# Norm steps and a bias addition of an attention stage put on GpSimd, the relu as one VectorE instruction

## The chip, the core and the metric

One core of one Trainium2 chip runs the whole program. Time is the device time of one execution in microseconds (us); the median of the runs counts. The core has five instruction queues: PE (TensorE, matmuls; PEld is its weight load), DVE (VectorE), ACT (ScalarE), POOL (GpSimd) and SP (SyncE, which here only issues transfers). Each runs its own queue in order and waits for the others by semaphores.

## The reference

Two layers. The first is a differential attention (8 heads of 16 rows of q and k, 4 batches of 512 tokens) beside a small attention over the batch and a mixture of 8 experts. The second is a four-layer state-space scan and a second mixture. The change touches only the first layer's attention and its experts. Of the experts it is this that matters:

```python
def _moe(x, Wg, W1, b1, W2, b2):
    ...
    idx = jnp.argmax(logits, axis=-1)
    for e in range(E):
        m = (idx == e)[:, None].astype(xf.dtype)
        h = jax.nn.relu(xf @ W1[e] + b1[e])
        out = out + m * (h @ W2[e] + b2[e])
```

The attention forms two softmaxes for each head, divides each by its sum of exponentials, weighs the second by minus lambda, adds the two and then normalizes by the root of the mean square over the head's 16 channels.

## The kernel before

The stage under study (`st2`, lines 631 to 1087) does two things at once. It walks through the 8 heads, and between the heads' steps it puts the 24 expert blocks of 128 tokens.

**Passes, units, steps.** `pair_of_heads` handles two heads in 32 steps. A unit is four steps, one batch of one head (512 queries against 4 x 128 keys), so there are eight units in a pass. The first pass has no expert blocks (it works out which tokens go to which block, `route`); the next two run in a hardware loop (`Fori`) and the last one is unrolled. Each unit of these three passes has one expert block: 24 in all.

**A step.** PE computes `bank_d` (`difference`, L817) and the two halves of `bank_l` (`scores`, L822, L823); ACT makes the gate `gt` by a tanh (L932); DVE makes the two sums `tt` (L988, L989); ACT takes the exponentials of two steps at once into `ex` (L939). `bank_d` and `bank_l` have two buffers each.

**The rest of a unit.** PE weighs the values with the exponentials of the unit before (`weigh`, L863, into `bank_pv`), in two halves; ACT copies `bank_pv` into `pvs` (`keep`, L944); PE transposes it back (`turn`, L871); DVE sums it into `ybig` (`settle`, L996), and only then may PE begin the next values.

**An expert block.** SP loads the block's tokens; PE transposes them (L838); ACT copies them to `xbT` (L948); PE computes the hidden layer in four matmuls of 128 columns (`hidden`, L844, into `bank_e`); DVE does bias and relu into `hid` (`relu`, L1004); PE multiplies by the second matrix (`block_out`, L850, the stationary operand is `hid`); ACT copies the result out (L953) and SP stores it. The weights come by an indirect transfer that GpSimd issues two blocks ahead (`gather_weights`), once `block_out` is done with the buffer.

**The order** is written by hand, one queue per engine. In a unit PE's order is: transpose the block, first half of the values, two differences, `hidden`, scores, second half of the values, scores, two differences, `block_out`, scores, `turn`, scores. DVE has the four steps' sums with `settle` after the second and the relu after the fourth. GpSimd has the copies for the next head (`next_head`) and the gathers.

**The norm.** `norm_head` handles one finished head on DVE in six small steps, one after each of the steps 5 to 10 and 21 to 26 of a pass: reciprocal of the sums (L1053), times minus lambda (L1057), values times reciprocals (128x512, L1059), sum of the two halves (L1061), square (L1063), sum over the channels (L1065). Each waits on the semaphore `s_hn` for the one before. The stage after this one handles the last head.

**Loads of heads.** q and k of a head are stacked in the memory of two idle tiles, `XT` and `GATE`, by 12 transfers a head on SP (`load_part`, L107, L109).

Of the kernel before, what the change touches and what calls it, by code (L numbers as in the profile page):

```python
# [7 lines left out]
ALU = mybir.AluOpType  # L8
# [3 lines left out]
P = 128  # L12
# [35 lines left out]
def build_stages(nc, A, out):  # L48
    keep = ExitStack()
    with keep:  # L50
# [24 lines left out]
        with keep0:  # L75
# [556 lines left out]
            with st2:  # L632
# [44 lines left out]
                s_hn = sem("head_norm_steps")  # L677
# [9 lines left out]
                loaded = lambda q, k: q * (8 * PER) + 16 * (k // 2 + 1)  # L687

                with nc.Block() as block:
                    @block.sync  # L690
                    def _(sp):
# [52 lines left out]
                    def _(pool):  # L744
# [12 lines left out]

                        def next_head(q, i):
# [15 lines left out]
                        pool.sem_inc(s_cur, LEAD)  # L774
# [9 lines left out]
                        next_head(-1, 0)  # L784
                        next_head(-1, 1)

                        def turn(q, more):
# [190 lines left out]
                    def _(dve):  # L978
                        for s in (s_T, s_yb, s_relu):
                            dve.sem_inc(s, LEAD)  # L980
# [67 lines left out]
                        def norm_head(h, n, settled, done):  # L1048
                            seg = ybig[:, :, bass.ds(h * 34, 34)].rearrange("p t (s c) -> p t s c", s=2)
                            plus, minus = seg[:, :, 0, 0:16], seg[:, :, 1, 0:16]  # L1050
                            if n == 0:
                                dve.wait_ge(s_yb, settled)
                                nc.vector.reciprocal(rz[:, :, :].unsqueeze(3), seg[:, :, :, 16:17]).then_inc(s_hn, 1)  # L1053
                                return
                            dve.wait_ge(s_hn, done + n)
                            if n == 1:
                                nc.vector.tensor_scalar(rz[:, :, 1], rz[:, :, 1], neg_lam[:, :], None, ALU.mult).then_inc(s_hn, 1)  # L1057
                            if n == 2:
                                TT(seg[:, :, :, 0:16], seg[:, :, :, 0:16], rz[:, :, :].unsqueeze(3).broadcast_to([P, NT, 2, 16]), ALU.mult).then_inc(s_hn, 1)  # L1059
                            if n == 3:  # L1060
                                TT(plus, plus, minus, ALU.add).then_inc(s_hn, 1)  # L1061
                            if n == 4:
                                TT(ysq[:, :, :], plus, plus, ALU.mult).then_inc(s_hn, 1)  # L1063
                            if n == 5:
                                nc.vector.tensor_reduce(ms[:, :, bass.ds(h, 1)], ysq[:, :, :].unsqueeze(2), AX.X, ALU.add).then_inc(s_hn, 1)  # L1065

                        def pair_of_heads(q, first=False):
                            for st in range(STEPS):
# [4 lines left out]
                                if 5 <= st < 11 and not first:  # L1073
# [1512 lines left out]
```

## Time and profile before

| | |
|---|---|
| median of 3 runs | 1316.74 us (1316.6 to 1319.15) |
| the profiled execution | 1318.12 us |
| its span | 1316.3 us |
| PE, DVE, ACT, POOL busy | 87%, 84%, 79%, 69% of the span |
| mean granted clock of PE | 0.953 |
| POOL in the slices of 33 us from 165 to 329 us | 1 tenth |

The span runs from the first to the last instruction of the program; the profiled execution's own time has what lies around it too. Busy shares are means over stages with different limits; the attention stage fills some 104 to 342 us. In the rows below a time stands from the span's start; "idle before" is the idle time of that engine just ahead of the row, and the name behind the arrow is what ended it.

### The profile page before, as it was taken

Reading aid. Unit: us, or ns where it says so; the run is one execution under the profiler, and the core shown is the slowest. Engines: PE = TensorE matmul, PEld = TensorE weight load, DVE = VectorE, ACT = ScalarE, POOL = GpSimd, SP = SyncE. Lnnn points to the kernel's source line nnn. Section 1 sums busy time; section 2 is a strip of 40 time slices with the busy share of each in tenths; the row PEclk is TensorE's granted clock in tenths of the full one; section 3 lists DMA queues with packets and bytes.
Section 4 is the critical chain, followed back from the end, with each engine's and each line's share of the span. In section 5 each row is a group of like instructions: output and inputs, shape, how many; then the busy total and the mean of one; then the engine's idle time right before and its main releaser. Section 6 shows DMA issues by size and latency. Waiting matters only on the chain. (4 is left out here: it accounts for less than half of the span.)

```text
span 1316.3 us, 21647 instructions
## 1 busy us (share of the span) xinstructions
PE 1145.7 (87%) x6667; PEld 611.3 (46%) x6667; DVE 1101.3 (84%) x1535; ACT 1043.2 (79%) x1804; POOL 912.4 (69%) x749
## 2 busy tenths in 40 slices
PE   6566799999719999977999999999999999999885
PEld 4461244444515656753444444444444444444442
DVE  8967899999675323339999999999999999999997
ACT  4346999999452224378999999999999999999992
POOL 6733311111473451367999999999999999999995
PEclk9786999999858999998999999999999999999998
DMA  2022233433108216434144414442442354234420
GB/s 71 33 88 95 77 107 113 126 114 104 31 23 287 88 36 163 129 85 101 54 107 106 99 45 104 104 98 56 104 112 68 74 107 113 59 77 105 107 65 16
DMA packets 89060, 120.19 MB, mean 91 GB/s; under 512 B 17869, under 2 KB 49464, under 8 KB 88576
## 3 DMA queue, kind: packets, MB, share of 16 engines
q1 hardware_dynamic: 82688, 101.59, 30.4%
q0 software_dynamic: 6272, 17.38, 4.5%
q8 instruction: 48, 0.79, 0.3%
q14 instruction: 52, 0.43, 0.1%
HBM read 92.28 MB, written 27.45 MB: 91 GB/s over the span
## 5 line engine op out<-in xcount | busy, mean ns | idle before, releaser
L2104 POOL TENSOR_TENSOR hcm<-hs,Cc 128x1024 f32<-128x1024 f32 x255 | 600.3, 2376 | 27.8 <-DVE hs L2487 19.8
L2487 DVE TENSOR_TENSOR_SCAN hs<-decay,dbx 128x512 f32<-128x512 f32 x512 | 586.9, 1201 | 25.6 <-ACT decay L2380 9.9
L2221 PEld LDWEIGHTS dbx<-ident_sb,scaled 128*128 128x128 f32 x2048 | 227.4, 142 | 288.7 <-DVE hs L2487 164.8
L2221 PE MATMUL dbx<-ident_sb,scaled 128*128 128x128 f32 x2048 | 312.1, 283 | 41.6 <-DVE hs L2487 38.2
L2362 ACT ACTIVATE scaled<-duT,BT 128x256 f32<-128x256 f32 x579 | 266.9, 506 | 0.2 <-PE dbx L2221 0.2
L2380 ACT ACTIVATE decay<-dtr_even,a_all 128x512 f32<-128x512 f32 x256 | 179.0, 723 | 3.0 <-DVE hs L2487 1.7
L2380 ACT ACTIVATE decay<-dtr_odd,a_all 128x512 f32<-128x512 f32 x256 | 177.7, 719 | 2.4 <-DMA dtr_odd<-dt_turn 1.5
L2239 PE MATMUL y_bank<-hcm,fold_sb 128*32 128x512 f32 x1024 | 138.9, 615 | 1.8 <-POOL hcm L2104 1.8
L939 ACT ACTIVATE ex<-tt 128x2048 f32<-128x2048 f32 x64 | 123.8, 1934 | 2.5 <-DVE tt L989 1.8
L2152 PE MATMUL slots<-XT,w_tap 128*128 128x512 f32 (+1 forms) x224 | 115.5, 597 | 3.1 <-DVE scaled L2478 2.9
L988 DVE TENSOR_TENSOR tt<-bank_l,gt 128x512 f32<-128x512 f32 x128 | 87.1, 681 | 12.7 <-ACT gt L932 10.9
L2089 POOL TENSOR_SCALAR scaled<-duT,BT 128x256 f32<-128x256 f32 x204 | 95.3, 479 | 0.0
L932 ACT ACTIVATE gt<-bank_d,dgh 128x512 f32<-128x512 f32 x128 | 82.7, 714 | 10.2 <-PE bank_d L817 9.2
L989 DVE SCALAR_TENSOR_TENSOR tt<-bank_l,gt 128x512 f32<-128x512 f32 x128 | 87.1, 680 | 0.0
L1849 DVE TENSOR_TENSOR hid<-sil,u_bank 128x512 f32<-128x512 f32 x32 | 22.0, 687 | 59.1 <-ACT sil L1706 37.5
L863 PE MATMUL bank_pv<-ex,v_head 128*32 128x512 f32 x512 | 69.1, 612 | 2.0 <-DVE ybig L996 1.7
L752 POOL CAST weight_rows<-w_row 128x1 uint32 (+1 forms) x24 | 4.7, 195 | 95.1 <-PE bank_e L850 95.1
L2478 DVE TENSOR_TENSOR scaled<-slots,BT 128x1024 f32<-128x1024 f32 (+1 forms) x60 | 67.9, 1131 | 0.0
L1706 ACT ACTIVATE sil<-g_bank 128x512 f32<-128x512 f32 x32 | 19.1, 597 | 47.3 <-PE u_bank L1563 47.2
L1939 DVE TENSOR_TENSOR hid<-sil,u_bank 128x320 f32<-128x320 f32 x32 | 15.6, 488 | 48.8 <-ACT sil L1792 48.8
L1527 POOL DMA_INDIRECT shares_of_tokens<-eo,to_u x18 | 17.2, 954 | 51.9 <-ACT eo L1829 48.3
L1519 POOL DMA_INDIRECT expert_rows<-XR,rows_u x32 | 31.3, 978 | 30.9 <-PE o_bank L1570 21.6
(379 smaller groups left out, 1882.3 us busy)
## 6 DMA issues: line engine op xcount, KB each, us to landing
Cc<-bc_turn SPq DMA_DIRECT2D x256, 64.0 KB, 2.2
dtr_even<-dt_turn SPq DMA_DIRECT2D x32, 512.0 KB, 8.7
dtr_odd<-dt_turn SPq DMA_DIRECT2D x32, 512.0 KB, 8.3
dt_turn<-dt SPq DMA_DIRECT2D x16, 512.0 KB, 2.8
hid<-in_conv_row SPq DMA_DIRECT2D x4, 512.0 KB, 5.4
shares_of_tokens<-zeros SPq DMA_DIRECT2D x2, 1024.0 KB, 7.9
w_rg<-in_w_rg SPq DMA_DIRECT2D x8, 256.0 KB, 3.0
w_ru<-in_w_ru SPq DMA_DIRECT2D x8, 256.0 KB, 3.8
```

Of the source, the lines that this page charges most:

```text
L932: nc.scalar.activation(gt[:, st % RING, :], bank_d[st % 2][:, :], ACT.Tanh, scale=dgh[:, i:i + 1]).then_inc(s_G, 1)
L939: nc.scalar.activation(ex[:, (st // 4) % 2, j:j + 2, :, :], tt[:, i:i + 2, :, :], ACT.Exp).then_inc(s_E, 2)
L988: nc.vector.tensor_tensor(tt[:, st % RING, 0, :], bank_l[st % 2][:, 0, :], gt[:, st % RING, :], ALU.add)
L989: nc.vector.scalar_tensor_tensor(tt[:, st % RING, 1, :], bank_l[st % 2][:, 1, :], -1.0, gt[:, st % RING, :], ALU.mult, ALU.subtract).then_ ...
L2089: nc.gpsimd.tensor_scalar(scaled[buffer_of(l, n, k)][:, kk, :, j, :], duT[:, n % 2, kk, :].rearrange("p (g c) -> p g c", c=32), BT[:, n % ...
L2104: nc.gpsimd.tensor_tensor(hcm[:, r - 1:r + 1, :], hs[:, p % HR - 1:p % HR + 1, :], Cc[:, k:k + 1, :].broadcast_to([P, 2, 512]), ALU.mult). ...
L2152: last = mm(dst[h][:, d:512], w_tap[:, 3 - d, P * h:P * h + P], XT[:, n % 4, 0:512 - d], start=(d == 0), stop=(d == 3))
L2221: last = nc.tensor.transpose(dbx[bank_of[p]][:, P * kk:P * kk + P], scaled[buffer_of(l, b, k)][:, kk, g, :, :].rearrange("p j c -> p (j c) ...
L2239: last = mm(y_bank[h][32 * q:32 * q + 32, :], fold[:, :], hcm[:, ring_of(l, b, p + q), :], start=False, stop=(k == 3), tile_position=(0, 3 ...
L2362: nc.scalar.activation(scaled[buffer_of(l, n, k)][:, kk, :, j, :], duT[:, n % 2, kk, :].rearrange("p (g c) -> p g c", c=32), ACT.Copy, sca ...
L2380: nc.scalar.activation(dec[:, p % DR, :], dtr[b % 2][:, g, :], ACT.Exp, scale=a_all[:, l, 4 * g + k:4 * g + k + 1]).then_inc(s_dec, 1)
L2487: nc.vector.tensor_tensor_scan(hs[:, p % HR, :], dec[:, p % DR, :], dbx[bank_of[p]][:, :], 0.0, ALU.mult, ALU.add).then_inc(s_sc, 1)
```

## The change

- **Relu.** `relu` was four DVE instructions of 128x128, each adding the bias (one number per partition) and taking the maximum with 0. Now `floor_at_bias` is one DVE instruction over 128x512: max(hidden, -b1), where the bias is spread along the innermost axis. A new GpSimd step `add_bias` adds b1 to it, in place. Since max(h, -b) + b = max(h + b, 0), the value is the same. `s_relu`, for which `block_out` waits, is now raised by GpSimd, and a new semaphore `s_floor` goes from DVE to GpSimd.
- **Norm.** Of the six steps DVE keeps the first and the last: `inverse_sums` at steps 5 and 21, `mean_square` at steps 14 and 30. The four between are `weigh_head` on GpSimd, after the add of the blocks k = 2 and k = 6, ahead of the gather.
- **SP.** The loads of the first head of the second pass stand ahead of the wait for the 16 scatters, and no longer behind it.

```diff
@@ sync
                         for part in range(2):
                             load_part(sp, 1, 1, part, s_ld[1])
+                        for part in range(2):
+                            first_head_of_next(-1, part)
                         sp.wait_ge(s_scat, 16 * NT)
                         for i in range(AHEAD):
                             load_block(i, i)
-                        for part in range(2):
-                            first_head_of_next(-1, part)
@@ gpsimd
+                        def weigh_head(h, done):
+                            seg = head_values(h)
+                            plus, minus = seg[:, :, 0, 0:16], seg[:, :, 1, 0:16]
+                            pool.wait_ge(s_hn, done)
+                            pool.sem_inc(s_asked, 1)
+                            nc.gpsimd.tensor_scalar(rz[:, :, 1], rz[:, :, 1], neg_lam[:, :], None, ALU.mult).then_inc(s_hn, 1)
...
+                            nc.gpsimd.tensor_tensor(seg[:, :, :, 0:16], seg[:, :, :, 0:16], rz[:, :, :].unsqueeze(3).broadcast_to([P, NT, 2, 16]), ALU.mult).then_inc(s_hn, 1)
...
+                            nc.gpsimd.tensor_tensor(plus, plus, minus, ALU.add).then_inc(s_hn, 1)
...
+                            nc.gpsimd.tensor_tensor(ysq[:, :, :], plus, plus, ALU.mult).then_inc(s_hn, 1)
...
                         next_head(-1, 0)
+                        weigh_head(0, 1)
                         next_head(-1, 1)
+
+                        def add_bias(q, k):
+                            pool.wait_ge(s_floor, blk(q, k + 1))
+                            pool.sem_inc(s_asked, 1)
+                            nc.gpsimd.tensor_tensor(hid[:, :, :], hid[:, :, :], b1[k % 2].unsqueeze(2).broadcast_to([P, 4, P]), ALU.add).then_inc(s_relu, 1)
 
                         def turn(q, more):
                             for k in range(PER):
+                                add_bias(q, k)
+                                if k == 2:
+                                    weigh_head(q * 2 + 1, q * 12 + 7)
                                 if k == PER // 2 and more:
                                     next_head(q, 0)
+                                if k == 6:
+                                    weigh_head(q * 2 + 2, q * 12 + 13)
                                 if more or k + AHEAD < PER:
@@ vector
-                        def relu(q, k):
+                        def floor_at_bias(q, k):
                             dve.wait_ge(s_h, blk(q, k + 1))
                             dve.wait_ge(s_wl[k % 2], loaded(q, k))
-                            for f in range(4):
-                                last = nc.vector.tensor_scalar(hid[:, f, :], bank_e[:, f, :], b1[k % 2][:, f:f + 1], 0.0, ALU.add, ALU.max)
-                            last.then_inc(s_relu, 1)
+                            nc.vector.scalar_tensor_tensor(hid[:, :, :], b1[k % 2].unsqueeze(2).broadcast_to([P, 4, P]), -1.0, bank_e[:, :, :],
+                                                           ALU.mult, ALU.max).then_inc(s_floor, 1)
...
+                                if st == 5 and not first:
+                                    inverse_sums(q * 2 + 1, unit(q, 0))
+                                if st == 14 and not first:
+                                    mean_square(q * 2 + 1, q * 12 + 11)
+                                if st == 21:
+                                    inverse_sums(q * 2 + 2, unit(q, 4))
+                                if st == 30:
+                                    mean_square(q * 2 + 2, q * 12 + 17)
                                 if mb == 3 and not first:
-                                    relu(q, u)
+                                    floor_at_bias(q, u)
```

DVE's queue in unit 1 of a pass in the loop, before. L988 and L989 are a step's sums, L1053 to L1059 the norm's first three steps, L1004 the relu; ISA and REGISTER_ALU rows make up addresses and wait values:

```order
L996 TENSOR_REDUCE ybig<-bank_pv 128x4x34
L1053 ISA
L1053 RECIPROCAL rz<-ybig 128x32
L985 REGISTER_ALU
L988 TENSOR_TENSOR tt<-bank_l,gt 128x512
L989 SCALAR_TENSOR_TENSOR tt<-bank_l,gt 128x512
L1055 ISA
L1057 TENSOR_SCALAR rz<-rz,neg_lam 128x16
...
L1059 TENSOR_TENSOR ybig<-ybig,rz 128x16x2x16
L1001 REGISTER_ALU
L1004 TENSOR_SCALAR hid<-bank_e,expert_weights 128x128 x4
```

The same place in the changed kernel, where L1018 and L1019 are the sums and L1033 is the new maximum:

```order
L1026 TENSOR_REDUCE ybig<-bank_pv 128x4x34
L1079 ISA
L1079 RECIPROCAL rz<-ybig 128x32
L1015 REGISTER_ALU
L1018 TENSOR_TENSOR tt<-bank_l,gt 128x512
L1019 SCALAR_TENSOR_TENSOR tt<-bank_l,gt 128x512
...
L1031 REGISTER_ALU
L1033 SCALAR_TENSOR_TENSOR hid<-expert_weights,bank_e 128x512
```

Two norm steps are gone from between the sums, and one instruction stands for the relu's four.

GpSimd's queue in the loop, before, from the gather of one block to the next (L752 casts the row numbers, L755 issues the transfer):

```order
L752 COPY weight_rows<-w_row 128x1
L753 REGISTER_ALU
L755 DMA expert_weights<-in_w_expert,weight_rows 128x1028
L752 ISA
L752 COPY weight_rows<-w_row 128x1
L753 REGISTER_ALU
L755 DMA expert_weights<-in_w_expert,weight_rows 128x1028
```

And in the changed kernel, from the add of block k = 2 to the gather behind it:

```order
L810 TENSOR_TENSOR hid<-hid,expert_weights 128x512
L763 ISA
L765 TENSOR_SCALAR rz<-rz,neg_lam 128x16
...
L768 TENSOR_TENSOR ybig<-ybig,rz 128x16x2x16
...
L771 TENSOR_TENSOR ybig<-ybig 128x16x16
L772 REGISTER_ALU
L774 TENSOR_TENSOR ysq<-ybig 128x256
L754 ISA
L754 COPY weight_rows<-w_row 128x1
L755 REGISTER_ALU
L757 DMA expert_weights<-in_w_expert,weight_rows 128x1028
```

An add now stands ahead of each gather, and behind two adds of a pass stand the norm's four middle steps.

## Rows read from the trace of the kernel before

**Rows 1.** Windows, 10 us: busy us (instructions) per engine, clock, DMA share, GB/s.

```profile
270.00:280.00 10.00, 9.94 (x72) 4.91 (x71) 9.46 (x21) 9.18 (x13) 1.20 (x2) 1.00 0.34 99
```

**Rows 2.** Timeline of PE, last pass: start, us, engine, line, operation, count, idle before.

```profile
283.35 1.05 PE L844 MATMUL bank_e<-block_inT,expert_weights 128*128 128x128 f32 x8
...
286.42 1.05 PE L850 MATMUL bank_e<-expert_weights,hid 128*128 128x128 f32 x8
...
290.36 1.06 PE L844 MATMUL bank_e<-block_inT,expert_weights 128*128 128x128 f32 x8
...
293.43 1.14 PE L850 MATMUL bank_e<-expert_weights,hid 128*128 128x128 f32 x8
```

**Rows 3.** Timeline of PE's weight loads, same stretch.

```profile
286.21 1.08 PEld L850 LDWEIGHTS bank_e<-expert_weights,hid 128*128 128x128 f32 x8
...
293.41 0.97 PEld L850 LDWEIGHTS bank_e<-expert_weights,hid 128*128 128x128 f32 x8 [0.31 <-DVE hid L1004]
```

**Rows 4.** Timeline of DVE, same stretch.

```profile
284.45 1.13 DVE L1004 TENSOR_SCALAR hid<-bank_e,expert_weights 128x128 f32<-128x128 f32 x4
...
288.90 0.35 DVE L1053 RECIPROCAL rz<-ybig 128x32 f32<-128x32 f32 x1
...
291.05 0.68 DVE L989 SCALAR_TENSOR_TENSOR tt<-bank_l,gt 128x512 f32<-128x512 f32 x1
291.64 0.68 DVE L1059 TENSOR_TENSOR ybig<-ybig,rz 128x512 f32<-128x512 f32 x1
292.24 1.12 DVE L1004 TENSOR_SCALAR hid<-bank_e,expert_weights 128x128 f32<-128x128 f32 x4
...
297.88 0.41 DVE L1065 TENSOR_REDUCE ms<-ysq 128x16 f32<-128x256 f32 x1
```

**Rows 5.** Timeline of ACT: its copy of bank_pv, one a unit.

```profile
153.93 0.78 ACT L944 ACTIVATE pvs<-bank_pv 128x512 f32<-128x512 f32 x1
161.95 0.60 ACT L944 ACTIVATE pvs<-bank_pv 128x512 f32<-128x512 f32 x1 [0.25 <-PE bank_pv L863]
...
263.94 0.60 ACT L944 ACTIVATE pvs<-bank_pv 128x512 f32<-128x512 f32 x1 [0.47 <-PE bank_pv L863]
271.66 0.60 ACT L944 ACTIVATE pvs<-bank_pv 128x512 f32<-128x512 f32 x1 [0.54 <-PE bank_pv L863]
278.78 0.60 ACT L944 ACTIVATE pvs<-bank_pv 128x512 f32<-128x512 f32 x1 [0.28 <-PE bank_pv L863]
...
292.80 0.60 ACT L944 ACTIVATE pvs<-bank_pv 128x512 f32<-128x512 f32 x1 [0.17 <-PE bank_pv L863]
300.60 0.60 ACT L944 ACTIVATE pvs<-bank_pv 128x512 f32<-128x512 f32 x1 [0.54 <-PE bank_pv L863]
```

**Rows 6.** POOL by line: duration ns min/median/max; the third from groups, busy and mean.

```profile
L386 POOL TENSOR_TENSOR prod<-mh x16: 1257/1268/1447, 20.4 to 42.0; 128x512 f32<-128x512 f32 x16
L393 POOL TENSOR_TENSOR prod<-mh,att x16: 1042/1046/1788, 47.5 to 80.2; 128x512 f32<-128x512 f32 x16
L1508 POOL TENSOR_TENSOR hid<-tap_in,hid 128x256 f32<-128x256 f32 x12 | 8.5, 737 | 20.0 <-DMA hid<-in_conv_row 20.0
```

**Rows 7.** Timeline of PE and POOL where the third pass begins.

```profile
226.23 1.06 PE L863 MATMUL bank_pv<-ex,v_head 128*32 128x512 f32 x8
227.99 1.05 PE L850 MATMUL bank_e<-expert_weights,hid 128*128 128x128 f32 x8
...
227.50 0.18 POOL L746 COPY dgh<-delta_gain_sb 128x1 f32 x1 [3.69 <-PE bank_pv L863]
227.63 0.39 POOL L749 COPY v_head<-v_tok 128x256 f32 x1
```

**Rows 8.** Timeline of SP and PE: the third head's loads and the wait for them.

```profile
143.01 1.91 SPq L107 DMA_DIRECT2D XT<-qk_parts  x3
...
159.96 0.61 PE L817 MATMUL bank_d<-XT 112*128 112x512 bf16 x2 [2.27 <-DMA XT<-qk_parts]
```

**Rows 9.** Timeline of PE in the last unit of the last pass.

```profile
336.24 1.16 PE L850 MATMUL bank_e<-expert_weights,hid 128*128 128x128 f32 x8 [0.52 <-DVE hid L1004]
```

More of the change, by code:

```diff
@@ L687, in build_stages @@
                 loaded = lambda q, k: q * (8 * PER) + 16 * (k // 2 + 1)
+                head_values = lambda h: ybig[:, :, bass.ds(h * 34, 34)].rearrange("p t (s c) -> p t s c", s=2)
                 with nc.Block() as block:
@@ L756, in gather_weights @@
                                                          bounds_check=NE * P - 1, oob_is_err=False).then_inc(s_wl[i], 16)
+                        def weigh_head(h, done):
[4 more added lines that the diff above has]
+                            nc.gpsimd.tensor_scalar(rz[:, :, 1], rz[:, :, 1], neg_lam[:, :], None, ALU.mult).then_inc(s_hn, 1)
+                            pool.wait_ge(s_hn, done + 1)
+                            pool.sem_inc(s_asked, 1)
+                            nc.gpsimd.tensor_tensor(seg[:, :, :, 0:16], seg[:, :, :, 0:16], rz[:, :, :].unsqueeze(3).broadcast_to([P, NT, 2, 16]), ALU.mult).then_inc(s_hn, 1)
+                            pool.wait_ge(s_hn, done + 2)
+                            pool.sem_inc(s_asked, 1)
+                            nc.gpsimd.tensor_tensor(plus, plus, minus, ALU.add).then_inc(s_hn, 1)
+                            pool.wait_ge(s_hn, done + 3)
+                            pool.sem_inc(s_asked, 1)
+                            nc.gpsimd.tensor_tensor(ysq[:, :, :], plus, plus, ALU.mult).then_inc(s_hn, 1)
                         def next_head(q, i):
@@ L773, in _ @@
                         nc.gpsimd.memset(zeros[:, :, :], 0.0).then_inc(s_zz, 1)
-                        pool.sem_inc(s_cur, LEAD)
+                        for s in (s_cur, s_relu):
+                            pool.sem_inc(s, LEAD)
                         pool.wait_ge(s_rows, 1)
@@ L978, in _ @@
                     def _(dve):
-                        for s in (s_T, s_yb, s_relu):
+                        for s in (s_T, s_yb, s_floor):
                             dve.sem_inc(s, LEAD)
@@ L1046, in route, with inverse_sums, mean_square @@
                                 link(nc.vector.tensor_scalar(w_row[:, :], w_row[:, :], lane[:, 0:1], None, ALU.add), s_rows)
[L1048 to L1065, printed above, removed]
+                        def inverse_sums(h, settled):
+                            dve.wait_ge(s_yb, settled)
+                            nc.vector.reciprocal(rz[:, :, :].unsqueeze(3), head_values(h)[:, :, :, 16:17]).then_inc(s_hn, 1)
+                        def mean_square(h, done):
+                            dve.wait_ge(s_hn, done)
+                            nc.vector.tensor_reduce(ms[:, :, bass.ds(h, 1)], ysq[:, :, :].unsqueeze(2), AX.X, ALU.add).then_inc(s_hn, 1)
                         def pair_of_heads(q, first=False):
@@ L1072, in pair_of_heads @@
                                     settle(q, u - 2)
-                                if 5 <= st < 11 and not first:
-                                    norm_head(q * 2 + 1, st - 5, unit(q, 0), q * 12 + 6)
-                                if 21 <= st < 27:
-                                    norm_head(q * 2 + 2, st - 21, unit(q, 4), q * 12 + 12)
+                                if st == 5 and not first:
[6 more added lines that the diff above has]
+                                    mean_square(q * 2 + 2, q * 12 + 17)
                                 if mb == 3 and not first:
-                                    relu(q, u)
+                                    floor_at_bias(q, u)
                                 if first:
```

3 lines of the change are left out of this document (2 added, 1 removed).

## The prediction

> **What bounds the kernel now.** I read the page first: 1316.3 us of span, most of it in the scan stage, which the change doesn't touch. The change lies in the attention stage, some 104 to 342 us. The windows view comes next: from 270 to 280 us PE, DVE and ACT are all over 90% busy and POOL is nearly idle, with the clock at full speed (2.4 GHz) [rows 1]. Busy shares can't say which of the three is the bound, so I took the timelines of the engines over whole units (a unit is four steps and one expert block; 24 units have a block). The period of a unit is read from ScalarE's copy of `pvs`, once a unit: 7.12 us in a plain unit inside the loops (271.66 to 278.78), 7.01 in the unrolled last pass (283.35 to 290.36 by PE [rows 2]), 7.72 and 7.80 where the norm's middle steps run [rows 5]. In the plain units ScalarE waits 0.28 or 0.17 us for PE, so its own work is 6.84 us. PE's rows stand end to start there [rows 2]. So **PE, in its written order, is the bound of a plain unit**, and DVE is what delays it in the units with norm steps. The six heads handled in the block loops cost, over plain units, 0.19 + 0.60 us each in the loops (the idle of 0.47 against 0.28, then 7.72 against 7.12) and 0.79 in the last pass (7.80 against 7.01) [rows 5]: 6 x 0.79, **4.8 us in all**. That is all that DVE's load costs now.
>
> **The relu.** Today `hidden` ends at 283.35 + 1.05 = 284.40, the relu starts at 284.45, and `block_out` loads its first weights at 286.21 [rows 2 to 4]. PE fills the 1.76 us from 284.45 to 286.21 with other work, so the relu may take that long for nothing; it takes 1.13 and leaves about 0.6. That PE feels it once this is gone shows at 292.24: a relu that started late ends at 293.36, PE loads `hid` at 293.41, 0.05 later and 0.02 ahead of the matmul instead of 0.21, and the block's matmuls take 1.14 us instead of 1.05 [rows 2 to 4].
> The new path is one DVE instruction over 128x512 with one operand in PSUM, 0.68 as the row of L989 [rows 4]; the hand-over to GpSimd; its add; and 0.05 to PE. The hand-over lies between 0.05 (DVE to PE above) and 0.21 (PE's values end at 227.29, GpSimd starts at 227.50, with a register address to make up first) [rows 3, 4, 7]; the add's addresses are fixed, but a semaphore instruction stands ahead of it, so 0.13. For a two-input 128x512 GpSimd operation there are two rows: 1.05 in the median where one operand is broadcast along the innermost axis (L393), 1.27 where none is (L386) [rows 6]. The bias is broadcast like the first, so 1.05; 1.27 stays as the upper end. Path: 0.68 + 0.13 + 1.05 + 0.05 = **1.91 us against 1.76 of cover**: 0.15 us of new waiting on PE in each plain unit. DVE is 0.44 us quicker, but it then waits for PE's transposes as before, and PE doesn't get it back.
> The Trainium skill (GPSIMD Engine Reference, section Engine selection) puts two-input elementwise work on GpSimd at about twice VectorE's time, which speaks against this change. The rows give 1.5 to 1.9 times. By that rule the add would take 1.36 us and the sum below be 7.4 us more.
> The long case of L393, 1.79 us, would hurt more [rows 6]. The skill (SBUF — State Buffer, section Who interferes with whom) says that a VectorE instruction with two SBUF inputs blocks a GpSimd one that reads SBUF. By that rule the add runs clear, since what DVE keeps in this stage has one input in PSUM, or only one input.
>
> **GpSimd's queue.** In the first block of each of the three passes with blocks, `next_head(…, 1)` stands ahead of the add in the queue; it waits for PE's values of the last unit. At the start of the third pass its copies run from 227.50 to 228.02 [rows 7]. The add then ends at 229.07, PE starts 229.12, while the load was due at 227.99 - 0.21 = 227.78: 1.35, three times, **4.1 us**. The gather of weights stands behind the add and, at k = 2 and 6, behind `weigh_head` too: 0.2 (as the small copy [rows 7]) + 1.05 + 2 x 0.74 [rows 6] and four hand-overs make some 3.3 us. That leaves GpSimd more than 2 us of a unit's 7.1 for the gather's cast and descriptors ahead of the next add. I take it that no add and, two blocks ahead, no block is delayed; a rival below has the price if one is.
>
> **The norm.** Four of six steps leave DVE; the reciprocal (0.35) stays in units 1 and 5, the reduction (0.41) moves to units 3 and 7. Starts follow 0.08 sooner than ends (291.05 + 0.68 against 291.64), so they take 0.27 and 0.33. They used to be partly covered by the 0.6 us; that cover is gone, and they now push the floor itself. Reciprocal: DVE would be free for it at 291.64, while `hidden` ended at 291.42, ready 0.05 later: 0.17 late, in each of six units [rows 2, 4]. In the four of them inside loops the 0.19 of today stays too. Reduction: 0.33 late in six units [rows 4]. `weigh_head` ends about 3.3 us after `block_out` starts, and the reduction wants it after 3.8: no wait, with little to spare.
>
> **The tail.** In the last unit no scores stand between: `block_out` waits for the relu, PE starts at 336.24 [rows 9], and transposes, settling and the last values follow. There all of 1.91 - 1.12 - 0.05 = 0.74 counts, and the reduction's 0.33: 1.07.
>
> **SP.** The loads of the third head into `XT` are now issued ahead of the wait for the scatters. They used to start at 143.01, and PE stood 2.27 us for them, until 159.96 [rows 8]. They need step 15 of the first pass; the copy at 153.93 belongs to its unit 6, so step 15 is over some three units of 6.5 us earlier, by 135. Eight us sooner hides the wait. That unit took 8.02 (153.93 to 161.95 [rows 5]) against ScalarE's 6.84 less two block copies, some 6.5: **1.5 us back**, between 0 and 2.27. The block loads behind them start no later than 144 or so and are wanted after 160.
>
> **Sum.** New waits over the 24 blocks: nine plain units (24 less 3 first, 6 with the reciprocal, 6 with the reduction) 9 x 0.15 = 1.35; four reciprocal units in loops 4 x (0.15 + 0.17 + 0.19) = 2.04, two in the last pass 0.64; five reduction units 5 x 0.48 = 2.4; three first units 4.1; tail 1.07: 11.6. Gone: 4.8 and 1.5. Net **+5.3 us**. The profiled execution took 1318.12 with a span of 1316.3; the median of the runs shown is 1316.74, and the sum holds for it as well: **1322.0 us**. By the skill's factor alone it would be 1329.4.
>
> **Rivals.**
> *The add hides.* If the whole path is 1.76 us or less (an add of 0.9, or a quicker hand-over), the 0.15 goes in all 24 units: 11.6 - 3.6 - 6.3 = +1.7, 1318.4. For it: the path rests on three estimates of a few hundredths. Against: no row of GpSimd at this size is under 1.04.
> *The add is slow.* At 1.27, 24 x 0.22 = 5.3 more: 1327.3. A `weigh_head` that holds up the reduction by a microsecond, five times, would give 5 more as well.
> *PE isn't the bound.* The ends of matmuls are modelled, so a gapless PE may hide slack. Then DVE's relief counts and the unit falls to ScalarE's 6.84: 16 x 0.28 + 8 x 0.17 = 5.8, with 4.8 and 1.5 makes 12.1: **1304.6**, faster. It decides where `block_out` could start without harm over 0.3 us later than today. Against it: the late relu at 293.36 lengthened PE's block at once [rows 2, 3].
> *The change does little* beside SP's move: that is close to the first rival and counted there.
>
> **How the numbers follow.** Forecast (0.05 to 0.25 us per plain unit, 1319.5 to 1324.5) 0.45; slow add or late reduction 0.2; the add hides 0.25; PE not the bound 0.1. A measurement here tells about 0.2%, 2.6 us, from no change. Faster 0.1, within 0.2% 0.25, slower 0.65. The range takes in the first two rivals with a margin for SP's 0 to 2.27 and leaves out the last: 1316.0 to 1329.0.
>
> **What would show it.** Right: PE idle before `block_out`, released by POOL, some 0.15 us in plain units and over 1 us in each pass's first; an add of 1.05; units of 7.2 to 7.6 us; no wait for `XT` near 158 us; stage 3 starting some 5 us later. Wrong: periods under 7.12 (PE had slack), an add with no one waiting for it, an add over 1.2, or DVE idle before the reduction for POOL.

## The result

The changed kernel takes 1321.23 us in the median of ten runs (1319.79 to 1322.98), the kernel before 1318.09 us in ten (1316.6 to 1320.92). The ratio is 1.0021, with a 95% interval of 1.0011 to 1.0031: slower by 2.8 us, between 1.4 and 4.1. The prediction was +5.3 us: the right side and well inside its range, but about twice too large. The absolute forecast, 1322.0 us, looks closer to 1321.23 than it was: it stands on a median of 1316.74 in three runs of the kernel before, and in ten runs that is 1318.09.

| | before | after |
|---|---|---|
| span of the profiled execution | 1316.3 us | 1318.7 us |
| DVE busy | 1101.3 us | 1081.9 us |
| POOL busy | 912.4 us | 956.2 us |
| first to last copy of `pvs` | 218.22 us | 220.77 us |

DVE lost 19 us of work and the program got longer. The last line is the measure I use from here on: ScalarE copies `pvs` once a unit, so the time from the first of these copies to the last covers the stage, and it doesn't move with what happens before or behind it. In the kernel before it runs from 122.14 to 340.36 us. Each span comes from one profiled execution. In units that no edit touches the time from copy to copy repeats to 0.03 us from kernel to kernel (6.35 to 6.38 in the first pass); only the unit where the second pass hands over to the third scatters more, 7.35 to 7.53 us in the kernels with the old or no bias step. So a difference between two spans is good to 0.1 or 0.2 us. These are ScalarE's copies in the timeline of the changed kernel (start, duration, engine, line, idle before), which answer to [rows 5]:

```profile
121.60 0.60 ACT L974 ACTIVATE pvs<-bank_pv 128x512 f32<-128x512 f32 x1 [0.65 <-PE bank_pv L893]
...
153.41 0.78 ACT L974 ACTIVATE pvs<-bank_pv 128x512 f32<-128x512 f32 x1
159.77 0.82 ACT L974 ACTIVATE pvs<-bank_pv 128x512 f32<-128x512 f32 x1
...
271.94 0.60 ACT L974 ACTIVATE pvs<-bank_pv 128x512 f32<-128x512 f32 x1 [0.37 <-PE bank_pv L893]
279.24 0.60 ACT L974 ACTIVATE pvs<-bank_pv 128x512 f32<-128x512 f32 x1 [0.45 <-PE bank_pv L893]
286.37 0.60 ACT L974 ACTIVATE pvs<-bank_pv 128x512 f32<-128x512 f32 x1 [0.29 <-PE bank_pv L893]
294.57 0.60 ACT L974 ACTIVATE pvs<-bank_pv 128x512 f32<-128x512 f32 x1 [0.56 <-PE bank_pv L893]
301.71 0.60 ACT L974 ACTIVATE pvs<-bank_pv 128x512 f32<-128x512 f32 x1 [0.29 <-PE bank_pv L893]
308.81 0.60 ACT L974 ACTIVATE pvs<-bank_pv 128x512 f32<-128x512 f32 x1 [0.25 <-PE bank_pv L893]
...
336.77 0.60 ACT L974 ACTIVATE pvs<-bank_pv 128x512 f32<-128x512 f32 x1 [0.74 <-PE bank_pv L893]
342.37 0.60 ACT L974 ACTIVATE pvs<-bank_pv 128x512 f32<-128x512 f32 x1 [2.65 <-PE bank_pv L893]
```

The unit that used to wait for `XT` takes 6.36 us (153.41 to 159.77) instead of 8.02. A plain unit of the last pass takes 7.10 (301.71 to 308.81) instead of 7.01. The unit behind the last pass's first block takes 8.20 (286.37 to 294.57), and the last one 5.60 (336.77 to 342.37), where it was 4.58. Now the two blocks of the last pass that are shown in part, PE, its weight loads, DVE and POOL, from their timelines, which answer to [rows 2 to 4] and, for the pass's first block, to [rows 7]:

```profile
286.51 0.18 POOL L748 COPY dgh<-delta_gain_sb 128x1 f32 x1 [3.22 <-PE bank_pv L893]
286.64 0.39 POOL L751 COPY v_head<-v_tok 128x256 f32 x1
287.01 1.03 POOL L810 TENSOR_TENSOR hid<-hid,expert_weights 128x512 f32<-128x512 f32 x1
...
288.09 1.16 PE L880 MATMUL bank_e<-expert_weights,hid 128*128 128x128 f32 x8 [0.93 <-POOL hid L810]
...
292.13 1.06 PE L874 MATMUL bank_e<-block_inT,expert_weights 128*128 128x128 f32 x8
...
293.28 0.68 DVE L1033 SCALAR_TENSOR_TENSOR hid<-expert_weights,bank_e 128x512 f32<-128x512 f32 x1
...
294.14 1.03 POOL L810 TENSOR_TENSOR hid<-hid,expert_weights 128x512 f32<-128x512 f32 x1 [2.74 <-DVE hid L1033]
...
295.23 0.97 PEld L880 LDWEIGHTS bank_e<-expert_weights,hid 128*128 128x128 f32 x8 [0.36 <-POOL hid L810]
...
295.23 1.16 PE L880 MATMUL bank_e<-expert_weights,hid 128*128 128x128 f32 x8
```

The new path stands here link by link. The maximum runs from 293.28 to 293.96, the add starts at 294.14, 0.18 later, and ends at 295.17, and PE loads `hid` at 295.23, released by POOL (the release stands on the row of the weight load; the matmuls' own row shows no idle time). In the pass's first block the copies for the next head come first; the add starts only at 287.01, and PE stands 0.93 us.

### The profile page after: what moved, and what is told of

Read it like the earlier page. It is cut to its first block and busy times, and to the rows that moved or that the text cites. A ratio compares the mean times of both kernels' runs of the same rounds, so it can differ in the third digit from the quotient of the medians.

```text
span 1318.7 us, 21654 instructions
## 1 busy us (share of the span) xinstructions
PE 1146.8 (87%) x6667; PEld 607.4 (46%) x6667; DVE 1081.9 (82%) x1435; ACT 1043.2 (79%) x1804; POOL 956.2 (73%) x801
## 5 line engine op out<-in xcount | busy, mean ns | idle before, releaser
L1018 DVE TENSOR_TENSOR tt<-bank_l,gt 128x512 f32<-128x512 f32 x128 | 87.1, 680 | 11.5 <-ACT gt L962 9.8
L1019 DVE SCALAR_TENSOR_TENSOR tt<-bank_l,gt 128x512 f32<-128x512 f32 x128 | 87.0, 679 | 0.0
L810 POOL TENSOR_TENSOR hid<-hid,expert_weights 128x512 f32<-128x512 f32 x24 | 24.9, 1036 | 49.0 <-DVE hid L1033 48.8
```

Of the source, the lines that this page charges most:

```text
L1018: nc.vector.tensor_tensor(tt[:, st % RING, 0, :], bank_l[st % 2][:, 0, :], gt[:, st % RING, :], ALU.add)
L1019: nc.vector.scalar_tensor_tensor(tt[:, st % RING, 1, :], bank_l[st % 2][:, 1, :], -1.0, gt[:, st % RING, :], ALU.mult, ALU.subtract).then_ ...
```

## Experiments

Ten kernels, each against runs of the kernel before on the same chip. "pvs span" is the time from the first to the last copy of `pvs` in the profiled execution. The medians move by 1 to 2 us between runs of one kernel; the pvs span shows what a single edit of a few tenths does.

| kernel | ratio to before (95%) | pvs span |
|---|---|---|
| before | 1 | 218.22 |
| the changed kernel | 1.0021 (1.0011 to 1.0031) | 220.77 |
| sp_only | 0.9991 (0.9982 to 1.0000) | 217.19 |
| relu_only | 1.0069 (1.0055 to 1.0083) | 225.81 |
| dose | 1.0040 (1.0027 to 1.0054) | 223.83 |
| no_asked | 1.0005 (0.9994 to 1.0016) | 218.81 |
| late_copies | 1.0000 (0.9991 to 1.0008) | 217.74 |
| split_late | 0.9964 (0.9950 to 0.9977) | 214.07 |
| norm_only | 0.9970 (0.9957 to 0.9983) | 213.58 |
| no_bias | 0.9959 (0.9944 to 0.9975) | 213.00 |
| norm_placed | 0.9952 (0.9939 to 0.9966) | 213.14 |
| vh_early | 0.9965 (0.9953 to 0.9978) | 212.45 |

My theory throughout: PE, in its written order, is the bound of the units with a block, with 1.76 us of other work between `hidden` and `block_out`; what comes back later than that is paid by PE in full. The rival: DVE's load counts, and so what leaves DVE is worth something by itself.

### The three parts one by one

**sp_only**: the kernel before, with SP's move alone.

```diff
+                        for part in range(2):
+                            first_head_of_next(-1, part)
                         sp.wait_ge(s_scat, 16 * NT)
                         for i in range(AHEAD):
                             load_block(i, i)
-                        for part in range(2):
-                            first_head_of_next(-1, part)
```

> The kernel before with SP's move alone: the third head's loads stand ahead of the wait for the scatters. The traces of before and after show the unit with the wait at 8.02 and at 6.36 us, and the next one at 6.52 and 7.14. If both come from the loads, the move gives back 1.66 - 0.62 = 1.0 us: 1.0 under the kernel before. If the 0.62 comes from GpSimd's part of the change, it gives 1.7. If the wait was harmless, 0.

The span fell by 1.03 us. The next unit takes 7.13 us here too, with no add on GpSimd, so the 0.62 belongs to the loads. What PE waits for instead stands in its timeline: after the first matmuls on `XT` it stands still for DVE's sums, which it didn't do there in the kernel before.

```profile
159.35 0.37 PE L822 MATMUL bank_l<-XT 48*128 48x512 bf16 x1 [0.39 <-DVE tt L989]
162.34 0.39 PE L822 MATMUL bank_l<-XT 48*128 48x512 bf16 x1 [0.53 <-DVE tt L989]
```

In this stretch, before the first block, PE isn't the bound. From 155 to 165 us ScalarE is busy 10.00 of 10 us and PE 8.18; in the kernel before ScalarE is busy 8.78, so the wait for `XT` had cost it 1.2. Of PE's wait of 2.27 us only 1.0 was to be had.

**norm_only**: the changed kernel with the relu of before on DVE.

```diff
-                            nc.vector.scalar_tensor_tensor(hid[:, :, :], b1[k % 2].unsqueeze(2).broadcast_to([P, 4, P]), -1.0, bank_e[:, :, :],
-                                                           ALU.mult, ALU.max).then_inc(s_floor, 1)
+                            for f in range(4):
+                                last = nc.vector.tensor_scalar(hid[:, f, :], bank_e[:, f, :], b1[k % 2][:, f:f + 1], 0.0, ALU.add, ALU.max)
+                            last.then_inc(s_relu, 1)
...
-                                add_bias(q, k)
```

> The changed kernel with the relu as before (four instructions on DVE, no add on GpSimd); the norm's middle steps stay on GpSimd, and SP's move stays. My theory (PE is the bound in its order, and DVE delays it only in norm units, where a relu of 1.12 us leaves 0.6 us of cover): the six heads' 4.8 us go, but for 0.19 us in four units where the reciprocal stands behind the settling, and SP's 1.0 comes on top: 5.0 us under before. Rival (GpSimd's norm steps cost something themselves, by its queue or by the shared SBUF port): 1 to 3 us under before.

The pvs span is 4.64 us under before (5.0 expected), and the ratio of 0.9970 says 4.0 (2.2 to 5.7). The ratio alone wouldn't part this from the rival's 1 to 3 us; the pvs span does. In the last pass every unit but the ends takes 7.01 us, the norm's units too. These are rows of this kernel, DVE's relu and PE's block, which answer to [rows 2, 4]:

```profile
287.52 1.12 DVE L1032 TENSOR_SCALAR hid<-bank_e,expert_weights 128x128 f32<-128x128 f32 x4
...
289.45 1.06 PE L878 MATMUL bank_e<-expert_weights,hid 128*128 128x128 f32 x8
```

The relu ends at 288.64 and PE's block starts at 289.45: cover left, and no release by anyone stands on PE's row. What it doesn't get is 0.32 us in the last unit (4.90 against 4.58): there the reduction stands ahead of a relu that PE is waiting for.

**relu_only**: the changed kernel with the norm's six steps on DVE as before (`norm_head` back, `weigh_head` gone).

```diff
-                                if k == 2:
-                                    weigh_head(q * 2 + 1, q * 12 + 7)
...
+                                if 5 <= st < 11 and not first:
+                                    norm_head(q * 2 + 1, st - 5, unit(q, 0), q * 12 + 6)
+                                if 21 <= st < 27:
+                                    norm_head(q * 2 + 2, st - 21, unit(q, 4), q * 12 + 12)
```

> The changed kernel with the norm's middle steps back on DVE; the relu stays one DVE maximum and an add on GpSimd. My theory: every us by which DVE starts the maximum late is a us for PE, since no cover is left. The product of the norm (0.60) and the small step (0.13) stand ahead of it in six units, so this is some 4 us slower than the changed kernel, about 7 over before. Rival (DVE is the bound, and the shorter relu frees 0.44 us of it in each unit): at or under the changed kernel's 1321.2.

The slowest of all: 1.0069, some 9 us over before by its runs, and 5.04 in the pvs span over the changed kernel, where 4 was expected. DVE and PE in unit 1 of the last pass:

```profile
299.34 0.68 DVE L1083 TENSOR_TENSOR ybig<-ybig,rz 128x512 f32<-128x512 f32 x1
299.94 0.68 DVE L1028 SCALAR_TENSOR_TENSOR hid<-expert_weights,bank_e 128x512 f32<-128x512 f32 x1
...
301.89 1.16 PE L875 MATMUL bank_e<-expert_weights,hid 128*128 128x128 f32 x8 [0.60 <-POOL hid L809]
```

The norm's product stands ahead of the maximum, and PE waits 0.60 us for the add, the very length of the product from start to start. The same norm steps cost 4.8 us with the old relu. So the two halves of the change are a gain and a loss: the norm's move is worth 3.6 us beyond SP's 1.03 (217.19 to 213.58), and the relu's costs 7.2 on top of that (213.58 to 220.77). The two aren't independent: taken in the other order, the relu's move costs 8.6 (sp_only to relu_only, 217.19 to 225.81) and the norm's is then worth 5.0.

### Is PE the bound?

**no_bias**: the changed kernel with the relu as one maximum with 0 on DVE and no add at all; the addition of b1 is left out.

```diff
-                            nc.vector.scalar_tensor_tensor(hid[:, :, :], b1[k % 2].unsqueeze(2).broadcast_to([P, 4, P]), -1.0, bank_e[:, :, :],
-                                                           ALU.mult, ALU.max).then_inc(s_floor, 1)
+                            nc.vector.tensor_scalar(hid[:, :, :], bank_e[:, :, :], 0.0, None, ALU.max).then_inc(s_relu, 1)
...
-                                add_bias(q, k)
```

> The changed kernel with the relu as one DVE instruction max(hidden, 0) and nothing on GpSimd: the bias b1 is left out, so this is a measuring kernel. DVE has 0.44 us less per block than with the relu of before (four instructions), and the path is far inside PE's cover. My theory (PE is the bound): from the first to the last copy of pvs as with the norm steps alone moved (213.6 us), less 0.4 in the last unit, so 1312 to 1313 us. Rival (PE's gapless rows hide slack and DVE's load counts): units fall from 7.12 and 7.01 towards ScalarE's 6.84, some 5 us less, 1307.

213.00 us against 213.58 for norm_only, the difference made in the last unit (4.46 against 4.90) and where the passes meet (7.40 against 7.53, no more than that unit's scatter). The plain units stay at 7.12 and 7.01. DVE has 0.44 us less to do in each of 24 blocks, and not one plain unit got shorter. The rival that PE's gapless rows hide slack has fallen: DVE's load in itself counts for nothing here.

**dose**: the changed kernel with a small GpSimd memset ahead of each add.

```diff
                             pool.sem_inc(s_asked, 1)
+                            nc.gpsimd.memset(spare[:, :], 0.0)
                             nc.gpsimd.tensor_tensor(hid[:, :, :], hid[:, :, :], b1[k % 2].unsqueeze(2).broadcast_to([P, 4, P]), ALU.add).then_inc(s_relu, 1)
```

> The changed kernel with one small GpSimd memset (128x128, 0.20 us busy in stage 2 of before, some 0.15 from start to start) ahead of each of the 24 adds. My theory: no cover is left, so each 0.01 us on the path counts in all 24 blocks: 24 x 0.15 = 3.6 us over the changed kernel, 1324.8. Rival (part of the path is still covered): under 1 us.

3.06 us more in the pvs span than the changed kernel. A plain unit of the last pass goes from 7.10 to 7.24, by 0.14, for a memset that takes 0.17 from start to start (291.54 to 291.71):

```profile
291.54 0.20 POOL L811 MEMSET spare<- 128x128 f32 x1
291.71 1.03 POOL L812 TENSOR_TENSOR hid<-hid,expert_weights 128x512 f32<-128x512 f32 x1
```

So four fifths of it are paid, and not in all 24 blocks. Twenty-one of them pay 0.13 to 0.22; the unit at the end of the second pass pays 0.06, and two of the last pass pay nothing: the one with its first reduction (7.30 us against 7.29) and the last unit (5.60 in both). There DVE's reduction stands ahead of the maximum, and where PE comes later the reduction delays it less: in the first of the two the maximum starts 0.10 us after `hidden` ends, in the changed kernel 0.24, in no_asked 0.33. That is most of what 3.06 us lacks to the 3.6 expected.

### What makes GpSimd's path long

**no_asked**: the changed kernel without the semaphore instruction between GpSimd's wait and its add.

```diff
                             pool.wait_ge(s_floor, blk(q, k + 1))
-                            pool.sem_inc(s_asked, 1)
```

> The changed kernel without the semaphore instruction that stands in GpSimd's queue between the wait for the maximum and the add. The hand-over was 0.19 us there, against 0.08 where stage 1 waits without it. My theory: it falls to about 0.12, the plain unit loses most of its 0.1 of new waiting, and 24 x 0.07 = 1.5 us go against the changed kernel. Rival (the hand-over is the same without it): no change.

The pvs span fell by 1.96 us (1.5 expected). DVE and POOL in this kernel:

```profile
300.70 0.69 DVE L1032 SCALAR_TENSOR_TENSOR hid<-expert_weights,bank_e 128x512 f32<-128x512 f32 x1
...
301.48 1.03 POOL L809 TENSOR_TENSOR hid<-hid,expert_weights 128x512 f32<-128x512 f32 x1 [2.61 <-DVE hid L1032]
```

The hand-over is 0.09 us (301.39 to 301.48) where it was 0.18 to 0.19. A plain unit of the last pass is back at 7.01, though the path is still 0.1 us over the cover (0.69 + 0.09 + 1.03 + 0.05 = 1.86); in the loops it takes 7.19, against 7.12 before. So one instruction that computes nothing was worth 2 of the changed kernel's 2.5 us.

**late_copies**: `next_head(…, 1)` behind the pass's first add.

```diff
-                        next_head(-1, 1)
...
                                 add_bias(q, k)
+                                if k == 0:
+                                    next_head(q - 1, 1)
...
-                            if more:
-                                next_head(q, 1)
```

> The changed kernel with the copies for the second head of a pass (the next_head with index 1) moved in GpSimd's queue from ahead of the pass's first add to behind it. In the changed kernel the three units with this queue are 1.07, 1.43 and 1.19 us longer than before, against 0.1 in plain units. My theory: they stand in the add's way, so this gives 3.4 us back and lands at about 0.5 us under before. Rival (the first unit is long because of the loop's turn itself): no change against the changed kernel.

The pvs span fell by 3.03 us to 0.48 under before, 0.5 expected; the ratio is 1.0000. The three first units take 7.49, 7.49 and 7.10 us where they took 8.38, 8.72 and 8.20, which is 3.22 less. The other units take 0.19 more in all: in the fifth of each loop pass (7.82 and 7.59 where it was 7.50 and 7.49) the add starts 0.51 and 0.29 us after the maximum's end, and the rows don't show for what. It wasn't the loop's turn but the queue: three copies of next to no work stood ahead of what PE was waiting for.

**split_late**: that, and the add in two halves, PE waiting for each.

```diff
-                            nc.gpsimd.tensor_tensor(hid[:, :, :], hid[:, :, :], b1[k % 2].unsqueeze(2).broadcast_to([P, 4, P]), ALU.add).then_inc(s_relu, 1)
+                            for f in (0, 2):
+                                nc.gpsimd.tensor_tensor(hid[:, f:f + 2, :], hid[:, f:f + 2, :], b1[k % 2][:, f:f + 2].unsqueeze(2).broadcast_to([P, 2, P]), ALU.add).then_inc(s_relu, 1)
...
-                            pe.wait_ge(s_relu, blk(q, k + 1))
                             for f in range(4):
+                                if f % 2 == 0:
+                                    pe.wait_ge(s_relu, LEAD + 2 * PER * q + (2 * k + f // 2 + 1))
```

> The changed kernel with the copies behind the first add (as in the run before) and the add in two halves of 128x256, each raising the semaphore, PE waiting for each half. The first half is there at 0.69 + 0.19 + 0.6 + 0.05 = 1.53 us after hidden, inside PE's 1.76, the second at about 2.1 where PE wants it at 2.26. My theory: the waits in plain units and in reductions go, so the same as with the norm steps alone moved (1312.6) but for some 0.5 in the last unit: 1313. Rival (the cost of using GpSimd is not the length of its add): at or over the 1319.0 of the run before.

214.07 us, 0.49 over norm_only. POOL and PE's weight load in the last pass:

```profile
289.10 1.18 POOL L810 TENSOR_TENSOR hid<-hid,expert_weights 128x256 f32<-128x256 f32 x2 [2.73 <-DVE hid L1034]
...
289.95 1.08 PEld L881 LDWEIGHTS bank_e<-expert_weights,hid 128*128 128x128 f32 x8
```

The weight load starts at 289.95, while the second half is still being added (289.10 + 1.18 = 290.28), and nothing holds it: 1.08 us for the eight, as in [rows 3] at 286.21. The last unit takes 5.38 against 4.90 and one unit with a reduction 7.08 against 7.01; the others are as in norm_only. So outside the last unit the add costs next to nothing once its first half is inside the cover.

### A better order

**norm_placed**: norm_only, with the reciprocal one step later and, in the last pass, the last reduction behind the relu.

```diff
-                                if st == 5 and not first:
+                                if st == 6 and not first:
                                     inverse_sums(q * 2 + 1, unit(q, 0))
...
-                                if st == 21:
+                                if st == 22:
                                     inverse_sums(q * 2 + 2, unit(q, 4))
...
-                                if st == 30:
+                                if st == 30 and not final:
                                     mean_square(q * 2 + 2, q * 12 + 17)
...
+                                if st == 31 and final:
+                                    mean_square(q * 2 + 2, q * 12 + 17)
```

> The kernel with the norm steps alone moved and the relu as before, with its two DVE steps placed otherwise: the reciprocal one step later, not right behind the settling (which PE waits for), and in the last pass the last reduction behind the relu. My theory: the 0.19 us that four units still have (7.31 against 7.12) and the 0.32 of the last unit (4.90 against 4.58) go: 1.1 us under the 1312.6 of that kernel, 1311.5. Rival (the 0.19 is no matter of place): no change.

Half right. The last unit is back at 4.59 us, but the units of 7.31 stayed at 7.29 to 7.34. The 0.19 us isn't the reciprocal's.

**vh_early**: that, and PE's wait for the value copies asked for only where its value changes, ahead of the block's transpose.

```diff
                                 pe.wait_ge(s_yb, unit(q, u))
-                                pe.wait_ge(s_vh, q * 2 + (3 + u // 4))
...
+                                if before and (u - 1) % 4 == 0:
+                                    pe.wait_ge(s_vh, q * 2 + (3 + (u - 1) // 4))
                                 if not first:
                                     turn_block(q, u)
```

> The kernel of the run before (norm steps alone moved, with the two DVE steps placed otherwise), and PE's wait for the head's values copy (s_vh) asked for only in units 1 and 5, ahead of the block's transpose instead of between the settling's signal and the values. The 0.19 us of these units (7.30 and 7.31 against 7.12) stayed when the reciprocal was moved, so it isn't the reciprocal. Theory: it is the register instruction for this second wait, which PE runs after the first is met. Then 4 x 0.19 = 0.8 us go, from 213.1 to 212.4 us between the first and the last copy of pvs. Rival (another cause, such as the copy itself being late): no change.

212.45 us, as expected, but not unit by unit. The fifth units of the two loop passes fall from 7.31 and 7.34 to 7.12, as expected; the first ones only from 7.30 and 7.29 to 7.20. Another 0.11 came where it wasn't expected, between the first pass and the second (7.13 to 7.02), and why isn't shown. The rows are from a fifth unit: PE's transposes back of `pvs`, the block's transpose and the values.

```profile
256.84 0.66 PE L898 MATMUL bank_pv<-ident_sb,pvs 128*128 128x128 f32 x4
...
257.75 0.33 PE L866 MATMUL bank_e<-ident_sb,block_in 128*128 128x128 f32 x1
258.14 1.06 PE L890 MATMUL bank_pv<-ex,v_head 128*32 128x512 f32 x8
```

From the transposes to the values it is 1.30 us here. In norm_placed the same two rows stand 1.52 apart:

```profile
257.06 0.66 PE L899 MATMUL bank_pv<-ident_sb,pvs 128*128 128x128 f32 x4
...
258.58 1.06 PE L891 MATMUL bank_pv<-ex,v_head 128*32 128x512 f32 x8 [0.28 <-DVE ybig L1024]
```

In norm_placed DVE's `settle` ends at 258.30 and the values start 0.28 later; in vh_early it ends at 258.08 and they start 0.06 later. The edit moves both a wait and the register instruction that makes up its value. The copy it waits for had been made four units earlier (at 226.72 in norm_placed), so it is the instruction, most likely; the run doesn't part the two. norm_only, norm_placed and vh_early all beat both kernels (0.9970, 0.9952, 0.9965); their runs, with intervals 0.0025 wide, can't rank them. By their pvs spans norm_placed is 0.44 us ahead of norm_only, 0.31 of it in the last unit, and vh_early 0.69 ahead of norm_placed.

## Why the prediction was right, and where its sizes were off

The mechanism held at each step that the timeline shows: PE bound in the units with a block, the path through GpSimd longer than its cover, the copies ahead of the first add, a tail that pays all. The sum was twice too large. By the time alone +2.8 us is nearer to the first rival ("the add hides", +1.7) than to the forecast; what decides is the timeline, with a path of 1.95 us and units that got longer by 0.09 to 0.19. By pvs intervals, after less before:

| term | predicted | measured |
|---|---|---|
| nine plain units | 1.35 | 1.35 |
| six reciprocal units (with the 0.19 in four) | 2.68 | 1.45 |
| five reduction units | 2.4 | 0.87 |
| three first units | 4.1 | 3.69 |
| tail | 1.07 | 1.02 |
| new waits | 11.6 | 8.4 |
| old norm waits gone | -4.8 | -4.8 |
| SP | -1.5 | -1.04 |
| net | +5.3 | +2.55 |

- **The path.** 1.91 us was forecast. It measures 0.68 + 0.18 + 1.03 + 0.06 = 1.95 at 293.28. The nine plain units paid 1.35 us, the forecast to the hundredth, and that was luck: 9 x 0.15 was forecast, three units of the last pass paid 0.09 each and six in the loops 0.17 to 0.19. Three things moved it. The hand-over, put at 0.13, was 0.18 to 0.19. In a loop the maximum starts 0.12 us after `hidden` ends (241.43 against 241.30), in a plain unit of the last pass 0.03 (300.36 against 300.33). And the first tenth of lateness is free. The step "1.91 against 1.76 of cover: 0.15" took the normal start of the weight load, 0.21 ahead of its matmul, for the last harmless one. These are the weight load and the matmuls of one plain unit of the last pass, in the changed kernel and in no_asked:

```profile
302.32 0.97 PEld L880 LDWEIGHTS bank_e<-expert_weights,hid 128*128 128x128 f32 x8 [0.32 <-POOL hid L810]
302.34 1.14 PE L880 MATMUL bank_e<-expert_weights,hid 128*128 128x128 f32 x8
...
302.56 0.98 PEld L879 LDWEIGHTS bank_e<-expert_weights,hid 128*128 128x128 f32 x8 [0.22 <-POOL hid L809]
302.68 1.06 PE L879 MATMUL bank_e<-expert_weights,hid 128*128 128x128 f32 x8
```

In both the matmuls start 2.01 us after `hidden` ends, as in the kernel before. With 0.12 us between the two rows the block takes its usual 1.06 us and the unit 7.01; with 0.02 it takes 1.14 and the unit 7.10. So the sign "PE idle before `block_out`, some 0.15 us in plain units" didn't come: the matmuls' row shows no idle time, only a longer block.
- **The reciprocal.** Of the terms this is the one that was plainly misread. "DVE would be free for it at 291.64" was read off the kernel before, where the small step L1057, which the change takes away, lay between (0.13 from start to start). Without it DVE is 0.04 late instead of 0.17; in the changed kernel the maximum starts at 293.28 with `hidden` ended at 293.19. The 0.19 of "today" in the four loop units did stay, as forecast, but it wasn't the reciprocal's (vh_early).
- **The reduction.** I counted all of 0.33 as late, because in the kernel before the relu and the end of `hidden` tie. In the changed kernel there is slack ahead of the maximum, since PE comes later and DVE doesn't; that PE's lateness and the reduction don't add up shows in dose, where 0.17 us on the path left the last pass's reduction unit and the last unit as they were. Inside a loop DVE waits 0.25 us for `hidden` in a plain unit; with the reduction ahead of it the maximum starts 0.08 after `hidden` ends (248.60):

```profile
241.43 0.69 DVE L1033 SCALAR_TENSOR_TENSOR hid<-expert_weights,bank_e 128x512 f32<-128x512 f32 x1 [0.25 <-PE bank_e L874]
...
247.54 1.06 PE L874 MATMUL bank_e<-block_inT,expert_weights 128*128 128x128 f32 x8
...
248.68 0.68 DVE L1033 SCALAR_TENSOR_TENSOR hid<-expert_weights,bank_e 128x512 f32<-128x512 f32 x1
```

- **First units and tail.** 3.69 and 1.02 us against 4.1 and 1.07. late_copies takes 3.22 of the first units' off again. In the last unit the path counts in full: the maximum starts 0.24 us later after `hidden` than the relu did, and PE 0.78 later after that, where 0.33 and 0.74 were forecast.
- **SP.** 1.0 instead of 1.5 us: the unit did give 1.66, but the estimate didn't ask what would hold PE next. It was DVE's sums behind a ScalarE without a gap, 0.39 and 0.53 us (sp_only).
- **The norm on GpSimd.** The estimate of 3.3 us for `weigh_head` was on the low side but harmless. In the third pass it runs from 243.32 to 246.77, 3.45 us, with 0.18 to 0.31 us ahead of each step, and the next add doesn't wait for it:

```profile
243.32 0.33 POOL L765 TENSOR_SCALAR rz<-rz,neg_lam 128x16 f32<-128x16 f32 x1
243.97 1.06 POOL L768 TENSOR_TENSOR ybig<-ybig,rz 128x512 f32 x1 [0.31 <-POOL rz L765]
245.30 0.68 POOL L771 TENSOR_TENSOR ybig<-ybig  x1 [0.27 <-POOL ybig L768]
246.16 0.61 POOL L774 TENSOR_TENSOR ysq<-ybig 128x256 f32 x1 [0.18 <-POOL ybig L771]
```

- **The add's length.** The Trainium skill (GPSIMD Engine Reference, section Engine selection) has about twice VectorE's time for it. The add took 1.03 to 1.05 us in all 24 blocks, 1.5 times DVE's 0.68 and not twice. No add took the long 1.79 us of [rows 6]: with no DVE instruction of two SBUF inputs left in the loops, the rule of the Trainium skill (SBUF — State Buffer, section Who interferes with whom) and these runs agree. They don't test it. Only in relu_only does such an instruction touch an add, in six blocks and for about 0.1 us (DVE's sum of the two halves starts at 301.74, the add ends at 301.83), and neither took longer than elsewhere.

## What to carry to other kernels

Where an engine with a fixed order is the bound, take from it the time between the instruction that frees a helper's step and the one that needs its result. That cover is the step's whole budget: a shorter step within it is worth nothing (no_bias), and a longer one costs most of its excess in nearly every round (dose). When work goes to an idle engine, send what nobody waits for (the norm, worth 3.6 us) and keep at home what the bound waits for (the relu, 7.2 us); if it must go, cut it so that the first piece comes in time (split_late). In the helper's queue look for bystanders ahead of the awaited step, copies and bare semaphore instructions both: three pairs of copies were worth 3.0 us here, and 24 semaphore instructions 2.0.

## What the runs showed of the hardware

- A semaphore instruction between a wait and the GpSimd instruction behind it costs 0.09 us: 0.18 us from DVE's end to GpSimd's start with it, 0.09 without it. I had put the whole hand-over at 0.13.
- A block of `block_out` whose weight load starts 0.02 us ahead of its matmuls takes 1.14 us instead of 1.06, and the unit grows by 0.09. With 0.12 us between them it takes 1.06 and the unit doesn't grow (no_asked); 0.21 is what it has when nothing is late.
- GpSimd adds in place with an operand spread along the innermost axis in 1.03 us for 128x512 and in 1.18 for two instructions of 128x256 back to back; cutting it in two costs 0.15 us, and each half takes 0.61 (split_late).
- Four loop units are 0.19 us longer than their neighbours; it was in plain sight in [rows 5] (0.47 against 0.28), and I put it down to DVE's reciprocal. Moving the reciprocal changed nothing (norm_placed). Moving one PE wait, and with it the register instruction that makes up its value, away from another wait took 0.19 to 0.22 us off two of the units and about 0.1 off the other two (vh_early).
